# Layer-norm rows and context transposed through DRAM and VectorE, not by TensorE

## The reference

```
h = layernorm(x);  x = attention(h, h) + x              # self-attention
h = layernorm(x);  x = attention(h, context) + x        # cross-attention
h = layernorm(x);  p = h @ ff_w1 + ff_b1
out = (p[:, :1024] * gelu(p[:, 1024:])) @ ff_w2 + ff_b2 + x
```

## Time and profile before

| | |
|---|---|
| median of 3 runs | 1751.52 us (1750.8 to 1753.15) |
| the profiled execution | 1751.38 us, span 1749.6 us |
| attention phase | up to about 1466 us of the span |
| feed-forward phase | about 1466 us to the end |
| PE, DVE, ACT, POOL busy | 99%, 82%, 68%, 61% of the span |
| DMA packets | 54.5% of 16 engines' span |
| granted TensorE clock | 0.999, at the upper level throughout |

### The profile page before, as it was taken

How to read it: one execution, slowest core, us unless ns; L and a number is a source line. 1 busy time by engine, 2 the same in 40 slices (tenths; PEclk the granted TensorE clock), 3 DMA queues, 4 the chain that set the end, 5 groups by cost and what they waited for, 6 DMA issues and landing times.

```text
span 1749.6 us, 43081 instructions
## 1 busy us (share of the span) xinstructions
PE 1723.8 (99%) x13824; PEld 1687.3 (96%) x13824; DVE 1440.9 (82%) x3137; ACT 1183.9 (68%) x3262; POOL 1059.3 (61%) x1791
## 2 busy tenths in 40 slices
PE   6999999999999999999999999999999999999998
PEld 6999999999999999999999999999999998888887
DVE  6888888888888888888888888888888897666664
ACT  5777777777777777777778777788777775221121
POOL 4787777766666666787777777666666664100100
PEclk9999999999999999999999999999999999999999
DMA  7776666666565555666667776666666661001000
GB/s 197 193 168 171 162 163 163 161 170 156 139 145 141 141 145 143 150 164 163 177 176 174 178 176 164 166 166 153 155 155 152 153 148 41 25 25 49 13 13 25
DMA packets 226496, 241.31 MB, mean 138 GB/s; under 512 B 68448, under 2 KB 190688, under 8 KB 226272
## 3 DMA queue, kind: packets, MB, share of 16 engines
q1 hardware_dynamic: 226272, 238.55, 54.5%
HBM read 58.08 MB, written 12.58 MB: 40 GB/s over the span
## 4 chain that ended last, share of the span: by engine, by line
PE 97%; DVE 1%; POOL 1%; issue 1%; ACT 0%; DMA 0%; DVEq 0%; POOLq 0%; ACTq 0%
PE QKB L294 20%; PE PVB L354 14%; PE PTB L340 13%; PE WOP L327 10%; PE VB L313 10%; PE S L261 7%; PE S L262 7%; PE S L758 5%; PE PTB L758 5%; PE VB L771 3%; PE QKB L771 3%; PE VB L236 1%; PE VB L249 0%; ACT PT L410 0%; PE PVB L737 0%
## 5 line engine op out<-in xcount | busy, mean ns | idle before, releaser
L410 ACT ACTIVATE PT<-S,NM 128x256 f32<-128x256 f32 x1024 | 471.8, 474 | 152.4 <-DVE NM L477 150.9
L465 DVE TENSOR_TENSOR PL<-PTB,PH 128x512 fp32r<-128x512 f32 x512 | 351.0, 686 | 152.9 <-ACT PH L429 149.2
L429 ACT ACTIVATE PH<-PTB 128x1024 fp32r<-128x1024 f32 x256 | 263.1, 1028 | 134.2 <-PE PTB L340 131.0
L656 POOL TENSOR_TENSOR ON<-ON,RB 128x256 f32<-128x256 f32 x256 | 188.4, 736 | 269.4 <-DVE ON L488 266.7
L477 DVE TENSOR_REDUCE NM<-S 128x2 f32<-128x512 f32 x512 | 326.3, 679 | 0.0
L340 PE MATMUL PTB<-IDN,PT 128*128 128x128 f32 x2048 | 266.1, 273 | 2.3 <-DVE PL L465 2.3
L261 PE MATMUL S<-RX 128*128 128x256 f32 x1024 | 256.9, 283 | 2.1 <-ACT PT L410 2.1
L262 PE MATMUL S<-RX 128*128 128x256 f32 x1024 | 256.8, 283 | 0.0
L340 PEld LDWEIGHTS PTB<-IDN,PT 128*128 128x128 f32 x2048 | 229.7, 140 | 3.2 <-DVE PL L465 3.2
L327 PE MATMUL WOP<-WO,OT 128*128 128x256 f32 x1536 | 226.5, 283 | 0.9 <-POOL OT L661 0.8
L294 PE MATMUL QKB<-HT,WA 128*128 128x256 f32 x1536 | 211.8, 288 | 6.6 <-POOL HT L561 3.6
(11 more groups left out here) (113 smaller groups left out, 3133.6 us busy)
## 6 DMA issues: line engine op xcount, KB each, us to landing
RX<-QKS SPq DMA_DIRECT2D x512, 192.0 KB, 2.9
RX<-QKS SPq DMA_DIRECT2D x512, 128.0 KB, 2.8
RB<-denominators SPq DMA_DIRECT2D x512, 64.0 KB, 2.6
out_dram<-XR SPq DMA_DIRECT2D x32, 256.0 KB, 3.0
XR<-in_x_dram SPq DMA_DIRECT2D x16, 256.0 KB, 3.1
denominators<-RDT SPq DMA_DIRECT2D x256, 16.0 KB
XR<-out_dram SPq DMA_DIRECT2D x16, 256.0 KB, 3.0
XN<-in_ctx_dram SPq DMA_DIRECT2D x16, 192.0 KB, 2.8
```

Of the source, the lines that this page charges most:

```text
L410: last = e.activation(PT[:, c % 2, j * S:(j + 1) * S], S1[:, i, qt * S:(qt + 1) * S], ACT.Exp, bias=NM[:, j:j + 1], accum_out=DEN[:, c % 2 ...
L429: e.activation(PH[:, s % 2, :], PTB[:, :, :].rearrange("p i n -> p (i n)"), ACT.Copy) \
L465: e.tensor_tensor(PL[:, cols], PTB[:, i, :], PH[:, s % 2, cols].bitcast(F32), ALU.subtract).then_inc(a.dve_pl, 1)
```

## The change

All of TensorE's transposes of rows and context go, but those for sequence 0. `XN` and `HF` change roles from sequence to sequence (`near`, `far`).

- Rows: DVE normalizes sequence seq+2 in pair 7 into `near`. SP stores it to a DRAM buffer `HS` in pair 0 (one DMA, 256 KB). ACT's queue loads it back in pair 1 as four DMAs of 32 partitions, in runs of 512 bytes; they move 32-row blocks to where the transpose wants them. DVE turns each 32x32 block in pair 2 (one instruction, 128x512). ACT applies gain and bias in pairs 3 and 4, POOL splits in pairs 3 and 4.
- Context: ACT's queue loads it for seq+2 in eight DMAs (three in pair 3, three in pair 4, two in pair 5), in runs of 128 bytes; DVE turns it in pair 6 (one instruction, 128x512); POOL splits it in pair 7 and pair 0.
- Stats move to pair 4, the aggregate to pair 5, the reciprocal root to POOL's pair 5; POOL's weight splits move from pairs 4 to 7 to pairs 2, 5, 6, 7.
- Feed-forward: aggregate at f=1, normalization at f=2; SP issues two stores and eight loads per chunk; DVE turns at f=4 and f=5 (two instructions each); ACT's gain and bias wait for both turns. For chunk 0 SP's two stores follow slot ATT-6's ring copies, its eight loads follow those of ATT-5, and DVE's turns end slots ATT-5 and ATT-4. POOL's last bias moves behind all attention slots.

```diff
-            if prepares:
-                n = seq + 1
-                if pair in (0, 1) and n >= B or pair in (2, 3):
-                    sl.wait(e, a.dve_vf, c + 1)
-                if pair in (0, 1) and n >= B:
-                    pe_ctx(e, sl, n, pair)
-                if pair in (2, 3):
-                    pe_h(e, sl, n, pair - 2)
+        def load_turned(e, dst, src, done, *parts):
+            for q in parts:
+                e.dma_start(dst[q * 32:(q + 1) * 32, :].rearrange("j (b f) -> j b f", b=4),
+                            src[:, q * P:(q + 1) * P].rearrange("(b j) f -> j b f", b=4)).then_inc(done, 16)
+
+        def act_load_rows(e, n, *parts):
+            e.wait_ge(d_hs, 16 * n)
+            e.wait_ge(a.pl_ht, 2 * n)
             if n >= B:
+                e.wait_ge(a.pl_ct, 2 * (n - B + 1))
+            load_turned(e, far(n), HS[0, :, :], d_hl, *parts)
+
+        def act_load_ctx(e, n, *pieces):
+            e.wait_ge(a.dve_th, n - 1)
+            src = ctxt[sequence(n), :, :]
+            for piece in pieces:
+                k, part = divmod(piece, 4)
+                col = k * P + (part - k * 2 * (part // 2)) * 32
+                e.dma_start(near(n)[part * 32:(part + 1) * 32, k * S:(k + 1) * S].rearrange("j (g i) -> j g i", i=32),
+                            src[:, col:col + 32].rearrange("(g j) i -> j g i", j=32)).then_inc(d_cx, 16)
...
@@ act_slot: between the copies of ON and the exponentials
+            if prepares:
+                if pair == 1:
+                    act_load_rows(e, seq + 1, 0, 1)
+                if pair in (3, 4):
+                    act_gain_bias(e, seq + 1, pair - 3)
+            if pair in (3, 4, 5) and sl.has(PAIRS * (seq + 2)) and seq + 2 >= B:
+                act_load_ctx(e, seq + 2, *range(3 * (pair - 3), min(3 * (pair - 2), 8)))
...
@@ act_slot: behind the copy of PH
+            if prepares and pair == 1:
+                act_load_rows(e, seq + 1, 2, 3)
...
+        def dve_turn_rows(e, n):
+            e.wait_ge(d_hl, 64 * n)
+            e.transpose(near(n).rearrange("p (g b j) -> p g b j", g=2 * TT, b=4),
+                        far(n).rearrange("p (b g i) -> p g b i", b=4, g=2 * TT)).then_inc(a.dve_th, 1)
+
+        def dve_turn_ctx(e, n):
+            e.wait_ge(d_cx, 128 * (n - B + 1))
+            e.wait_ge(a.pl_ht, 2 * n)
+            e.transpose(far(n), near(n)).then_inc(a.dve_tc, 1)
...
@@ dve_slot
+            if prepares and pair == 2:
+                dve_turn_rows(e, seq + 1)
+            if pair == 6 and sl.has(PAIRS * (seq + 2)) and seq + 2 >= B:
+                dve_turn_ctx(e, seq + 2)
+            if pair == 7 and sl.has(PAIRS * (seq + 2)):
+                dve_normalize(e, sl, a, seq + 2, (near(seq + 2),))
...
+        def dve_ffn_turn(e, chunk, h):
+            e.wait_ge(d_fl, 128 * (chunk + 1))
+            for k in range(KD):
+                last = e.transpose(ROWS[k][:, h * S:(h + 1) * S].rearrange("p (t b j) -> p t b j", t=TT, b=4),
+                                   TURNED[h].rearrange("p (b k t i) -> p k t b i", b=4, k=KD, t=TT)[:, k])
+            last.then_inc(fs.dve_th, 1)
...
@@ dve_ffn
                     dve_stats(e, sl, fs, chunk + 1)
+                    dve_aggregate(e, sl, fs, chunk + 1)
                 if f == 2:
+                    dve_normalize(e, sl, fs, chunk + 1, ROWS)
+                if f in (4, 5):
+                    dve_ffn_turn(e, chunk + 1, f - 4)
...
@@ SP
+            def load_ffn_rows(chunk):
+                e.wait_ge(d_fs, 32 * (chunk + 1))
...
+                for h in range(2):
+                    load_turned(e, TURNED[h], HS[1 + h, :, :], d_fl, 0, 1, 2, 3)
...
+                if pair == 0 and 0 <= seq < 2 * B - 1:
+                    store_rows(seq + 1)
+                if c == ATT - 6:
+                    store_ffn_rows(0)
+                if c == ATT - 5:
+                    load_ffn_rows(0)
```

More of the change, by code:

```diff
@@ L123, in block_kernel, with near, far @@
         WOP = pb("WOP", [P, 512])
-        CX = XN[:, :].rearrange("p (t s) -> p t s", t=TT)
         DS = nc.dram_tensor("denominators", (4, 32, P), F32, kind="Internal").ap()
+        def near(n):
+            return (XN if n % 2 else HF)[:, :]
+        def far(n):
+            return (HF if n % 2 else XN)[:, :]
+        HS = nc.dram_tensor("rows", (3, P, XW), F32, kind="Internal").ap()
         def raw(n, half):
@@ L224, in block_kernel, with pe_first_rows @@
         attentions = (Attention(0, WA), Attention(1, WB))
[L227 to L234, removed]
+        def pe_first_rows(e, k, bank):
+            e.wait_ge(a.dve_xn, 1)
             for t in range(TT):
@@ L387, in act_slot @@
             seq, pair = divmod(c, PAIRS)
+            prepares = c >= 0 and sl.has(PAIRS * (seq + 1))
             if sl.has(c - 3):
@@ L708, in block_kernel @@
         OB = (QKB, VB)
-        def halves(chunk):
-            if chunk == 0:
-                return XN[:, :], HF[:, :]
-            return HF[:, :], RB[:, :, :].rearrange("p r s -> p (r s)")
-        def rows(chunk):
-            return (STG[:, 0:CW], STG[:, CW:2 * CW]) if chunk == 0 else halves(chunk)
-        def transposes(chunk):
-            return (QKB, QKB) if chunk == 0 else (PVB, WOP)
+        ROWS = (XN[:, :], HF[:, :])
+        TURNED = (STG[:, 0:CW], STG[:, CW:2 * CW])
         def w1(k, part, col):
@@ L729, in w2 @@
             return WA[:, 4 + f // 4, part, (f % 4) * D:(f % 4 + 1) * D]
-        def pe_ffn_h(e, sl, chunk, *ks):
-            sl.wait(e, fs.dve_xn, chunk + 1)
-            for k in ks or range(KD):
-                sl.wait(e, fs.act_hf, KD * chunk + (k if ks else 0))
-                for t in range(2 * TT):
-                    col = t % TT * D + k * P
-                    last = e.transpose(transposes(chunk)[k][:, t * P:(t + 1) * P],
-                                       halves(chunk)[t // TT][:, col:col + P], IDN[:, :])
-                last.then_inc(fs.pe_ht, 1)
         def pe_ffn(e, sl):
@@ L775, in pe_ffn, with act_ffn_h @@
                 last.then_inc(fs.pe_f2, 1)
-            if c >= 0 and c % PAIRS == 5 and sl.has(c + PAIRS):
-                if chunk == 0:
-                    e.wait_ge(a.dve_xo, 2 * B)
-                    e.wait_ge(a.dve_ad, ATT)
-                pe_ffn_h(e, sl, chunk + 1)
-        def act_ffn_h(e, sl, chunk, *ks):
-            for k in ks or range(KD):
-                sl.wait(e, fs.pe_ht, KD * chunk + k + 1 if ks else KD * (chunk + 1))
-                e.activation(rows(chunk)[k], transposes(chunk)[k][:, :], ACT.Identity,
-                             bias=LNG[:, 2, 1, k:k + 1], scale=LNG[:, 2, 0, k:k + 1]).then_inc(fs.act_hf, 1)
+        def act_ffn_h(e, chunk, k):
+            e.wait_ge(fs.dve_th, 2 * (chunk + 1))
+            e.activation(ROWS[k], ROWS[k], ACT.Identity, bias=LNG[:, 2, 1, k:k + 1],
+                         scale=LNG[:, 2, 0, k:k + 1]).then_inc(fs.act_hf, 1)
         def act_ffn(e, sl):
```

188 lines of the change are left out of this document (90 added, 98 removed).

## The result

The changed kernel takes 1756.64 us (median of 20 runs, 1751.76 to 1762.76), the kernel before 1752.05 us (20 runs, 1750.47 to 1753.83): ratio 1.0025, 95% interval 1.0016 to 1.0034. It is slower by a quarter of a per cent, where 12 us less was forecast. (The time lies within the stated 1722 to 1765 us, which the rivals had widened, but it moved the other way.)

A forecast was written before the change was run, and what follows sets the result against it. TensorE, busy 99% of the span and 97% of the chain, was taken as the bound. 1751.4 - 19.7 (attention) + 6.4 (feed-forward) + 0.9 (last attention slots) = 1739 us; own range 1731 to 1748, 8-in-10 range 1722 to 1765.

The forecast's parts named there:

- What TensorE gains: Removed transposes, 0.11 us each on the chain: 20.7 us in attention, 27.8 us in all with the feed-forward.
- In pair 1 ACT waits for the store: Attention, pair 1: row loads behind the store make exponentials up to 1.0 us late, under the 1.8 us to spare; cost 0.
- POOL. Cost 0: Attention, pair 5: weight splits and reciprocal root meet; POOL busy 34.9 of 44.33 us, so no cost beyond the 1 us allowance.
- lateness that meets by chance: Allowance of 1 us for the whole attention phase, making its sum -19.7 us.
- Rival 4: Gain and loss cancel: feed-forward at its upper bound plus some us of late store landings in pair 1, 1750 us; chance 0.1.
- ACT's issues: Attention, pairs 1, 3 and 4: DMA issues on ACT's queue at 0.6 us each delay exponentials under 1.8 us; cost 0.
- Rival 2: ACT's issues delay the exponentials in pairs 1, 3 and 4, from 1.1 us an issue; at 1.2 us, 1767 us; chance 0.15.
- Rival 3: DVE becomes the bound of cross-attention, from a turn of 1.35 us; at 1.9 us, 1757 us; chance 0.1.
- DMA: Cross sequences: added packets at most 27 ns each raise the DMA share from 0.70 to at most 0.78; cost 0.
- Rival 5: DMA engines fill and ring copies come late, from 96 ns an added packet; at twice that 1947 us; chance 0.02.
- Feed-forward: Late DRAM round trip: TensorE stands 1.8 us per chunk, 12.6 us in seven, against 6.2 gained: +6.4 us (0 to +13).
- Last slots: End of attention: DVE stands 3.8 us for chunk 0's loads, 3.3 us lost, against gains of 0.9 and 1.5: +0.9 us.

The follow-up runs named there:

- e1: Changed kernel with SP issuing the row store of pair 0 ahead of that iteration's four ring copies, not behind them: 1737.27 us.
- e5: Changed kernel with SP's row store one step later, in pair 1's iteration ahead of the ring copies: 1812.28 us.
- e9: Changed kernel with only POOL's quarters of the staged weights moved to pairs 3 to 6 instead of 2, 5, 6, 7: 1752.77 us.
- e3: Changed kernel with POOL's weight splits back in pairs 4 to 7, as before the change: 1760.17 us.
- e4: Changed kernel with DVE's turns of chunk 0 and ACT's gain and bias each one slot later in the last attention slots: 1756.62 us.

## Why the prediction was wrong, step by step

- **What TensorE gains: right.** 20.7 us in attention forecast, 20.4 found in undisturbed sequences; in the feed-forward 0.88 us a chunk forecast, 0.73 found (34.31 to 33.58).
- **"In pair 1 ACT waits for the store", at most 1.0 us late with 1.8 to spare: the step that failed.** Its times nearly hold in sequence 25: the store 2.4 us behind the start of pair 0's maxima (2.9 said), landed 5.4 us behind it (5.4 to 6 said), the exponentials 1.1 us late. But it took SP to be on time. In sequence 23 SP was 1.4 us later, since its spread waits for POOL's `ON`, the landing was 3.6 us and not the 2.5 taken from a quiet stretch (median 3.0 behind ring copies, at worst 4.4), and the exponentials came 2.4 us late. TensorE stood 1.1 us for that and the slot grew by 1.2, so there was 1.2 us to spare, not 1.8. The 1.8 was read in a slot without preparing steps, where the exponentials start 3.7 us ahead of the next scores; in pair 0 of sequence 25 of after they start 3.3 us ahead. That this wait costs the time is shown: e1 took it away (19 us less), e5 lengthened it (56 us more).
- **"POOL. Cost 0": wrong too**, as it looked at POOL's busy sum over a sequence (34.9 of 44.33 us), while what counts is which operation of a slot SP waits for. In sequence 23 the chain shows SP's spread waiting for POOL's `ON`. How large POOL's part is isn't shown: e9, which took the quarter out of pair 7, brought 3.7 us in the median and nothing in the profiled execution, and the 3.5 us of e3 stand beside longer landings, not a later POOL. How the 20.5 us divide between POOL, SP's own queue, the landing and the clock stays open, because they meet in the same slots.
- **The term of 1 us for "lateness that meets by chance"** is where this should have stood: 20.5 us in the profiled execution. Rival 4 (0.1) named late store landings in pair 1 and came near the time, but by a loss in the feed-forward that wasn't there.
- **ACT's issues: cost nothing, as forecast, though for less.** The median is 0.42 us for the loads of rows and 0.47 for those of context, where 0.6 was taken, and 43.36 us stand in sequences with all 12 issues. Rival 2 named pair 1 and the exponentials rightly, but by the wrong cause: not the issues' time delayed them but the landing that they wait for. Its condition, 1.1 us per issue, was met by 17 single issues of 252 and not by the median.
- **DVE: right.** A turn of 128x512 takes 0.70 us (0.7 taken), two of 128x256 0.85 added up (0.9). Rival 3 never came up.
- **DMA: right.** The stretch of the cross sequence in the earlier trace rows now has a share of 0.75, where at most 0.78 was forecast, and ACT's queue fills 3.4% of the engines' span with 52,672 packets: 0.034 x 1750 x 16 / 52,672 = 0.018 us a packet, where 27 ns was the bound taken. Rival 5 is out. The Trainium skill's page "DMA: Bandwidth & Descriptors", section Specifications, has a read-modify-write below 512 bytes; these 0.018 us a packet, over runs of 128 and 512 bytes together, show no price of it.
- **Feed-forward, +6.4 forecast, -3.9 found: the stall was mis-sized.** From T = 1581.93 of this chunk, normalization ends at T + 6.9, as said. The two stores took 0.34 and 0.43 us (0.55 taken), the loads began at T + 9.65 (10.2), took 0.53 each (0.57) and the turn started at T + 15.4, not 16.9. The 1.5 us are nearly all of the 1.8 forecast as a stall; 0 to 0.6 a chunk was left. Here the error helped, by 10 us, and that it hid half of the loss in attention is luck.
- **Last slots, +0.9 forecast, +4.1 found.** The wait of DVE was 3.5 us (3.8 said), the slot lost 4.2 (3.3 said), partly at the lower clock: four microseconds from 1449 have a mean of 0.57. The gains of 0.9 and 1.5 us that were set against it aren't to be seen: without this stall the seven distances would be 38.5, as before. A part is DVE's normalization, which makes the two slots that hold it long in every version: 5.84 and 5.97 us in after, 5.85 and 6.30 before. Why the rest of the gain doesn't show stays open.

Sum over the profiled executions: +0.1 (start) - 20.4 + 20.5 + 4.1 - 3.9 = +0.4, for a span that went from 1749.6 to 1750.0 us. The runs' medians are 4.6 apart, because the profile of after is at the fast end of its runs, and those with a lower mean clock lie above it.

## What to carry to other kernels

When an engine in the critical round waits for a transfer, write down the whole queue that the transfer's issue stands in and everything that queue waits for: a store that was thought to have 1.8 us to spare was late behind four ring copies and a GpSimd result that it has nothing to do with. A step with a deadline goes ahead of its neighbours in the queue that have more time, and in the last slots here eight loads went better in two groups of four. Read the time to spare in a slot of the kind that the step stands in. Read the landing time from a stretch with the same traffic, and test such a margin by a dose in both directions: one line moved each way gave -19 and +56 us.

## What the runs showed of the hardware

- A store of 256 KB landed a median of 3.0 us after issue behind four ring copies of the same queue, and 2.2 us ahead of them.
- A load of 32 partitions (64 KB) holds ACT's queue a median of 0.42 us and SP's 0.43; eight in a row on SP take 4.24 us. Halving the bytes of each didn't change it (8.42 us for 16), and single issues took up to 1.9 us.
- A stand of TensorE can cost more than its length: after one of 3.53 us its score matmuls took 0.42 us instead of 0.28 for a while (mean granted clock 0.57 over 1449 to 1453). After one of 2.08 us (e4) the clock also fell, after one of 2.21 us (e5, sequence 30) it did not, and after 1.1 us (after, sequence 23) it did not. The Trainium skill's page "TensorE: Matmul & The Clock Gate", section What's actually happening, says that the array's clock has only these two levels and follows how busy TensorE has recently been. The rows agree that it can fall after a stand, but the length of the stand alone doesn't decide it.
